# Attention passes of a four-layer graph network: TensorE signals aggregations once a quad, four-head query rows once for eight chunks, and transposed weights together with the factor

## The chip, the cores and the metric

One core of a Trainium2 chip runs the whole program. The metric is the device time of one execution in microseconds (us), lower is better. Engines are named as in the profile: PE is TensorE's matmul, PEld its weight load, DVE VectorE, ACT ScalarE, POOL GpSimd, SP SyncE.

## The reference

A graph with 3125 nodes of 256 features and 53125 edges sorted by destination (`dst`). Four graph layers, each followed by residual and layer norm: a plain sum over edges, two layers of graph attention with four heads, three layers of a graph transformer with eight heads, and a relational sum over edges. The change touches the five attention passes only:

```python
# four heads, two passes
e = leaky_relu(el[src] + er[dst])
ex = exp(e - segment_max(e, dst)[dst])
out = segment_sum(z[src] * (ex / segment_sum(ex, dst)[dst]), dst)
# eight heads, three passes
scores = sum(Q[dst] * typed(K[src]), -1) * mu / sqrt(32)
e = exp(scores - segment_max(scores, dst)[dst])
agg = segment_sum(V[src] * (e / (segment_sum(e, dst)[dst] + 1e-10)), dst)
```

## The kernel before

Edges lie in chunks of 128, one edge in each partition. `attend` handles a window of 16 chunks (`WC`) at a time: 28 windows with four heads ("sums" below, `dots` false), 29 with eight ("dots", `dots` true). A quad is four chunks. A unit is what is aggregated in one PSUM bank: one chunk in sums (16 units in a window, four in a quad, six banks `pp`), two in dots (8 units, two in a quad, three banks).

Window w goes through these steps:

- POOL gathers the table row of each edge by an indirect DMA, one for each chunk (L757), into a ring of windows. Before each quad it waits until the quad that held the place is aggregated (`s_pp`, L749 to L751).
- SP loads the destination rows that become one-hot matrices for eight chunks at a time (L741); ACT turns them into ones and zeros (L855, L858).
- PE brings the query row of each edge (`qrows`: L779 in sums, L785 in dots) and signals `s_q` once a quad. DVE makes scores: `leaky` in sums (L945 to L951), `dot` and `red` in dots (L931, L936).
- PE transposes the scores (`T1`, L793), DVE takes running maxima (`D1` to `D3`), PE makes differences (`below`, L797 and L798) and the ratio between windows (`ratio`, L802), ACT takes exponentials (`weights`, L881 and L882), PE transposes them back (`T5`, L807), and ACT copies them into the ring (L886 and L887 in dots, L889 in sums).
- PE makes the factor that rescales the running sum (`factor`, L813 to L815), ACT copies it (`factors`, L893), and T1 of the next window waits for that copy (`s_fc`).
- ACT makes one-hot matrices for the aggregation (`rows`, L864 and L869), DVE multiplies the gathered rows by the weights (`weigh`, L1010), PE aggregates unit by unit (`agg`, L828) and signals `s_pp` after each unit, and DVE rescales (L1000, L1001) and adds each unit to its tile (`add`, L1018).

All engines run rounds: round r aggregates window r-2, makes the weights of r-1 and the scores of r. The order inside a round is written by hand for DVE and PE. In the strings, for PE, C1 to C5 are `T1`, `below`, `ratio`, `T5` and `factor`, Q and N are query rows of a quad of this and of the next window, and G0 to G7 are eighths of the aggregation (two units in sums, one in dots). For DVE, S is `dot`, R `red`, W `weigh`, t the rescaling, A an add of this round's window, P an add of the window before, L `leaky`, and B a residual. `agg` waits on `s_acc` for a free bank.

A `then_inc` on the last matmul of a group is PE's signal; any engine waits for it with `wait_ge`. The first and the last stage of the program (`sum_edges`, L1144 for its indirect DMAs, L1193 for its matmuls) have the same kind of gather and aggregation without attention. Between the attention passes lie dense stages, in which POOL issues no indirect DMA.

## Time and profile before

| | us |
|---|---|
| median of three runs | 7191.65 |
| lowest and highest | 7173.81, 7196.2 |
| the profiled execution | 7153.48, its span 7151.4 |
| PE, DVE, ACT, POOL busy | 4511.4, 3873.4, 3586.2, 3942.8 |

A row of groups reads: line, engine, operation, output<-input, shape, count | busy us, mean ns of one | idle time of the engine just before them, and what ended it. A row of the timeline reads: start us, duration us, engine, line, operation, and in brackets how long the engine had sat idle. "issue" there means that the profile shows nothing that the engine waited for. "remote", or a DMA named by an old buffer, stands where a wait ended at a time at which no instruction that updates its semaphore had just ended.

### The profile page before, as it was taken

How to read it: one execution, taken by the hardware profiler on the slowest of the kernel's cores; microseconds unless marked ns; L12 is line 12 of the kernel's file. 1: busy time of each engine (PE TensorE's matmuls, PEld its weight loads, DVE VectorE, ACT ScalarE, POOL GpSimd, SP SyncE). 2: the span in 40 equal slices, each digit the busy share in tenths (PEclk: the TensorE clock that was granted, in tenths of full speed). 3: DMA queues.
4: the chain of work that ended last, by engine and by line, in shares of the span. 5: the costliest groups of instructions: out<-in, count | busy, mean ns of one | idle time of the engine just before them, and what ended most of it. 6: DMA issues, size and time to landing. Idle time of an engine off the chain costs nothing. (4 is left out here: it accounts for less than half of the span.)

```text
span 7151.4 us, 82528 instructions
## 1 busy us (share of the span) xinstructions
PE 4511.4 (63%) x22100; PEld 3453.4 (48%) x22100; DVE 3873.4 (54%) x9224; ACT 3586.2 (50%) x9073; POOL 3942.8 (55%) x3964
## 2 busy tenths in 40 slices
PE   5444355445556456655777895777895777895444
PEld 3344233323444244454555784555794555673332
DVE  7222223245667356675777445777545777663223
ACT  3333132334444444455666575666575666555554
POOL 0666566647773677535666225666225666215665
PEclk9555566666777676787888997888897888997666
DMA  1111233333432433336666326666326666423333
GB/s 60 44 50 55 62 97 94 90 94 108 110 109 63 115 108 110 90 125 196 196 193 193 90 79 192 195 195 194 91 79 185 192 194 193 114 89 118 92 90 90
DMA packets 395658, 864.23 MB, mean 121 GB/s; under 512 B 93353, under 2 KB 203851, under 8 KB 391763
## 3 DMA queue, kind: packets, MB, share of 16 engines
q0 software_dynamic: 209680, 608.73, 31.4%
q1 hardware_dynamic: 177296, 246.02, 10.3%
q10 hardware_dynamic: 8243, 4.30, 0.2%
q8 instruction: 193, 3.16, 0.2%
q14 instruction: 246, 2.02, 0.1%
HBM read 743.33 MB, written 115.44 MB: 120 GB/s over the span
## 5 line engine op out<-in xcount | busy, mean ns | idle before, releaser
L757 POOL DMA_INDIRECT ring<-tab_kv,idx_i x1044 | 1072.5, 1027 | 534.2 <-issue 295.7
L757 POOL DMA_INDIRECT ring<-tab_z,src_i x880 | 948.8, 1078 | 402.0 <-issue 243.2
L1193 PE MATMUL pp<-ring,oh 128*128 128x256 f32 x1760 | 609.0, 502 | 635.8 <-issue 268.6
L1018 DVE TENSOR_TENSOR acc<-acc,pp 128x264 f32 x1576 | 668.3, 424 | 470.9 <-PE pp L828 120.7
L1327 DVE TENSOR_TENSOR acc<-acc,pp 128x256 f32 x880 | 370.5, 421 | 889.2 <-DMA tab_z<-zs 280.4
L1193 PEld LDWEIGHTS pp<-ring,oh 128*128 128x128 f32 x1760 | 416.2, 251 | 829.1 <-issue 677.3
L828 PE MATMUL pp<-ring,scratch 128*128 128x264 f32 x1760 | 678.5, 526 | 114.2 <-issue 66.7
L785 PE MATMUL pq<-Qs,oht 128*128 x4176 | 620.5, 306 | 186.4 <-issue 98.2
L828 PE MATMUL pp<-ring,X 128*128 128x264 f32 x2088 | 667.4, 454 | 51.0 <-DVE acc L1018 32.0
L1010 DVE TENSOR_TENSOR ring<-ring 128x1024 f32<-128x1024 f32 x481 | 585.9, 1219 | 187.7 <-ACT ring L889 108.6
L785 PEld LDWEIGHTS pq<-Qs,oht 128*128 128x128 bf16 x4176 | 439.3, 109 | 346.6 <-issue 238.1
L638 POOL DMA_INDIRECT rec<-R,idx_i x416 | 408.2, 981 | 274.5 <-DVE idx_i L613 142.4
L1144 POOL DMA_INDIRECT ring<-tab_y,src_i x440 | 417.9, 950 | 237.5 <-issue 123.0
L1144 POOL DMA_INDIRECT ring<-tab_h,idx_i x440 | 420.6, 956 | 224.3 <-issue 121.4
L828 PEld LDWEIGHTS pp<-ring,scratch 128*128 128x128 f32 x1760 | 401.5, 255 | 256.1 <-issue 125.2
L855 ACT ACTIVATE oht<-oht,part_c 128x1024 bf16<-128x1024 bf16 x284 | 323.3, 1138 | 401.2 <-DMA oht<-lo_row_p 197.2
L931 DVE TENSOR_TENSOR X<-ring,pq 128x1024 f32<-128x1024 f32 x261 | 317.6, 1217 | 346.7 <-issue 252.4
L828 PEld LDWEIGHTS pp<-ring,X 128*128 128x128 f32 x2088 | 423.3, 223 | 157.2 <-issue 44.3
L757 POOL DMA_INDIRECT H<-tab_kv,idx_i x348 | 351.7, 1011 | 235.0 <-issue 84.6
L864 ACT ACTIVATE X<-iota_row,lo__40877 128x128 f32<-128x128 f32 x1392 | 424.1, 388 | 2.4 <-PE pp L828 2.4
L936 DVE TENSOR_REDUCE scw<-X 128x32 f32<-128x1024 f32 x348 | 422.9, 1215 | 0.8
L1685 POOL TENSOR_TENSOR R<-H,rows 128x256 f32<-128x256 f32 x75 | 66.0, 880 | 586.1 <-DVE H L2070 586.1
(363 smaller groups left out, 9421.3 us busy)
## 6 DMA issues: line engine op xcount, KB each, us to landing
oht<-lo_row_p SPq DMA_DIRECT2D x174, 256.0 KB
oht<-lo_row_s SPq DMA_DIRECT2D x110, 256.0 KB
drow<-in_dst SPq DMA_DIRECT2D x25, 1024.0 KB
tab_h<-hs SPq DMA_DIRECT2D x25, 1024.0 KB, 4.4
tab_kv<-X SPq DMA_DIRECT2D x50, 396.0 KB, 2.7
tab_kv<-X SPq DMA_DIRECT2D x50, 384.0 KB, 3.4
ring<-tab_kv,idx_i POOLq DMA_INDIRECT x1044
ring<-tab_z,src_i POOLq DMA_INDIRECT x880
```

The lines of the kernel that those rows point to most:

```text
L638: nc.gpsimd.indirect_dma_start(out=rec, out_offset=bass.IndirectOffsetOnAxis(ap=slot[:, j:j + 1], axis=0), in_=R[:, j, :], in_offset=None) ...
L757: nc.gpsimd.indirect_dma_start(out=one(w, c, 0, row), out_offset=None, in_=table, in_offset=bass.IndirectOffsetOnAxis(ap=idx[:, w * WC + c ...
L785: last = nc.tensor.matmul(o, lhs, Qs[:, bass.ds(tile_, 1), r, :].rearrange("p a d -> p (a d)"), start=(r == 0), stop=(r == 2))
L828: last = nc.tensor.matmul(pp[(w * NU + n) % NB][:, 0:W8], oh[:, w % 2, UC * n + c, :], one(w, UC * n + c, 0, W8), start=(c == 0), stop=(c ...
L855: nc.scalar.activation(oht[:, k % LOB, :], oht[:, k % LOB, :], ACT.Abs, scale=-1.0, bias=part_c[:, :]).then_inc(s_ac, 1)
L864: last = nc.scalar.activation(oh[:, w % 2, c, :], iota_row[:, :], ACT.Abs, scale=-1.0, bias=lo_s[:, w * WC + c:w * WC + c + 1])
L936: nc.vector.tensor_reduce(scw[:, w % 2, :, 4 * q:4 * q + 4].rearrange("p h c -> p c h"), prod[:, q % 2, :, :].rearrange("p c (h x) -> p c ...
L1010: nc.vector.tensor_tensor(v, v, bc(ex, 3, D // heads), ALU.mult).then_inc(s_m, 1)
L1018: nc.vector.tensor_tensor(a, a, pp[(w * NU + p) % NB][:, 0:W8], ALU.add).then_inc(s_acc, 1)
L1144: nc.gpsimd.indirect_dma_start(out=ring[:, b, k, c, :], out_offset=None, in_=table, in_offset=bass.IndirectOffsetOnAxis(ap=idx[:, 2 * p + ...
L1193: last = nc.tensor.matmul(bank[:, c * D:(c + 1) * D], oh[:, b, 2 * k + c, :], ring[:, b, k, c, :], start=True, stop=True)
L1327: nc.vector.tensor_tensor(a, a, pp[b % 2 * BP + k][:, c * D:(c + 1) * D], ALU.add).then_inc(s_v, 1)
```

## The change

PE signals `s_pp` after the last unit of a quad only: 4 times in a window instead of 16 in sums, instead of 8 in dots. Every waiter counts quads instead of units: POOL's gathers, ACT's `rows`, DVE's `add`. In sums `s_q` is signalled after every second quad. T5 does not signal any more, `factor` does not wait for ACT's copy, and ACT waits once, for the factor, then copies the transposed weights and the factor. `T5` and `factor` stand next to each other in PE's order, ahead of G5 in dots and of G6 in sums. In DVE's order for sums, four adds instead of six are left for the next round.

```diff
-    ORDER_V_SUMS = order("W0 P10 P11 W1 P12 P13 W2 P14 P15 t D1 A0 A1 D2 A2 A3 D3 A4 A5 W3 B A6 A7 A8 A9 L")
-    ORDER_T_DOTS = order("l C1 G0 Q2 G1 G2 Q3 G3 C2 C3 G4 C4 G5 C5 N0 G6 N1 G7")
-    ORDER_T_SUMS = order("l G0 C1 G1 Q0 Q1 G2 Q2 Q3 G3 G4 C2 C3 G5 C4 G6 C5 G7")
+    ORDER_V_SUMS = order("W0 P12 P13 W1 P14 P15 W2 t D1 A0 A1 D2 A2 A3 D3 W3 A4 A5 B A6 A7 A8 A9 A10 A11 L")
+    ORDER_T_DOTS = order("l C1 G0 Q2 G1 G2 Q3 G3 C2 C3 G4 C4 C5 G5 N0 G6 N1 G7")
+    ORDER_T_SUMS = order("l G0 C1 G1 Q0 Q1 G2 Q2 Q3 G3 G4 C2 C3 G5 C4 C5 G6 G7")
...
-                            e.wait_ge(s_q, 2 * (k - LOB + 1))
+                            e.wait_ge(s_q, (2 if dots else 1) * (k - LOB + 1))
...
-                                e.wait_ge(s_pp, (w + 3 - RW) * NU + QU * (q + 1))
+                                e.wait_ge(s_pp, (w + 3 - RW) * NQ + q + 1)
...
-                        last.then_inc(s_q, 1)
+                        if dots or q % 2:
+                            last.then_inc(s_q, 1)
...
-                        nc.tensor.transpose(ex_t, S1, ident[:, :]).then_inc(s_T5, 1)
+                        nc.tensor.transpose(ex_t, S1, ident[:, :])
                     def factor(w):
-                        e.wait_ge(s_ex, w + 1)
...
-                        last.then_inc(s_pp, 1)
+                        if n % QU == QU - 1:
+                            last.then_inc(s_pp, 1)
...
-                        e.wait_ge(s_pp, w * NU + HU * (h + 1))
+                        e.wait_ge(s_pp, w * NQ + NQ // 2 * (h + 1))
...
-                        e.wait_ge(s_T5, w + 1)
+                        e.wait_ge(s_fac, w + 1)
                         ex = ex_t.rearrange("p (h c) -> p c h", h=HD)
...
-                    def factors(w):
-                        e.wait_ge(s_fac, w + 1)
                         nc.scalar.copy(facs[:, w % 2, :], fac).then_inc(s_fc, 1)
...
-                        e.wait_ge(s_q, w * NQ + quads(w))
+                        e.wait_ge(s_q, 2 * w + quads(w) // 2)
...
-                        e.wait_ge(s_pp, w * NU + (p + 1 + 2 * NU))
+                        e.wait_ge(s_pp, (w + 2) * NQ + p // QU + 1)
```

## Rows read from the trace of the kernel before

**Rows 1.** The page: busy time of each engine over the whole span.

```profile
PE 4511.4 (63%) x22100; PEld 3453.4 (48%) x22100; DVE 3873.4 (54%) x9224; ACT 3586.2 (50%) x9073; POOL 3942.8 (55%) x3964
```

**Rows 2.** Windows: stretch, length, then PE, PEld, DVE, ACT, POOL busy, clock, DMA.

```profile
1640.00:2260.00 620.00, 382.74 (x1609) 267.82 (x1609) 396.92 (x1009) 303.93 (x680) 412.77 (x376) 0.74 0.39 103
3300.00:3960.00 660.00, 497.87 (x2530) 367.73 (x2529) 508.96 (x945) 409.24 (x1163) 431.63 (x421) 0.83 0.69 192
```

**Rows 3.** Windows, POOL alone: gathers of two sums, one dots, the last stage.

```profile
1560.00:2229.00 669.00, 471.38 (x436) 0.70 0.41 109
2337.00:3001.00 664.00, 472.89 (x440) 0.69 0.41 111
3236.00:3948.00 712.00, 472.53 (x464) 0.81 0.69 194
6479.00:7100.00 621.00, 413.92 (x433) 0.66 0.32 91
```

**Rows 4.** Groups of POOL's gathers: sums, dots (two), last stage.

```profile
L757 POOL DMA_INDIRECT ring<-tab_z,src_i x436 | 471.4, 1081 | 192.3 <-issue 121.1 <-remote 41.4 <-PE pp L828 29.9
L757 POOL DMA_INDIRECT ring<-tab_kv,idx_i x348 | 356.2, 1024 | 184.7 <-issue 99.9 <-DMA keep_link<-link_p 38.8 <-POOLq L150 17.8
L757 POOL DMA_INDIRECT H<-tab_kv,idx_i x116 | 116.4, 1004 | 72.6 <-issue 28.6 <-PE pp L828 25.7 <-DMA keep_link<-link_p 15.2
L1144 POOL DMA_INDIRECT ring<-tab_h,idx_i x425 | 406.3, 956 | 219.7 <-issue 117.2 <-DMA tab_z<-zs 74.5 <-SPq L1097 15.5
```

**Rows 5.** Timeline of one round of sums, from the ratio on.

```profile
1838.71 0.20 PE L802 MATMUL pc<-G,one_c 128*1 128x8 f32 x2
1838.84 1.16 PE L828 MATMUL pp<-ring,scratch 128*128 128x264 f32 x4
...
1847.57 0.95 POOL L757 DMA_INDIRECT ring<-tab_z,src_i  x1 [0.30 <-issue]
1850.08 0.28 ACT L881 ACTIVATE scratch<-pc 128x128 f32<-128x128 f32 x1 [8.54 <-remote]
...
1850.45 0.48 PE L807 MATMUL pc<-ident,scratch 128*128 128x128 f32 x1 [10.46 <-issue]
...
1851.62 1.69 POOL L757 DMA_INDIRECT ring<-tab_z,src_i  x1 [3.10 <-remote]
```

**Rows 6.** Timeline of one round of sums, the factor and its copy.

```profile
1723.26 0.57 PE L815 MATMUL pc<-gr,scratch 1*128 1x8 f32 x2
...
1732.79 0.17 ACT L893 COPY facs<-pc 128x8 f32<-128x8 f32 x1 [10.46 <-remote]
```

**Rows 7.** Timeline of a dense stage, where POOL issues no indirect DMA.

```profile
4100.09 1.03 PE L1716 MATMUL pbe<-Wo,xa 128*128 128x256 f32 x4
...
4101.16 0.42 DVE L2011 TENSOR_TENSOR H<-pbe,H 128x256 f32<-128x256 f32 x1 [2.45 <-PE pbe L1716]
```

**Rows 8.** Timeline of one round of dots around the factor.

```profile
3461.03 1.73 PE L828 MATMUL pp<-ring,X 128*128 128x264 f32 x4
...
3462.74 0.42 DVE L1018 TENSOR_TENSOR acc<-acc,pp 128x264 f32 x1
...
3463.06 0.38 PE L813 MATMUL pc<-one_r 1*128 1x8 f32 x2 [0.30 <-issue]
3463.08 1.22 DVE L936 TENSOR_REDUCE scw<-X 128x32 f32<-128x1024 f32 x1
...
3463.53 0.36 PE L815 MATMUL pc<-gr,X 1*128 1x8 f32 x2
...
3468.46 0.17 ACT L893 COPY facs<-pc 128x8 f32<-128x8 f32 x1 [5.46 <-DMA keep_x<-H]
3468.49 0.43 DVE L1018 TENSOR_TENSOR acc<-acc,pp 128x264 f32 x1 [4.20 <-DMA keep_link<-link_p]
```

More of the change, by code:

```diff
@@ L724, in attend @@
             ratio_row, fac = pc[0:1, 3 * P:3 * P + HD], pc[:, 3 * P + HD:3 * P + 2 * HD]
-            (s_go, s_oh, s_ev, s_q, s_mul, s_red, s_T1, s_G, s_Gm, s_eg, s_T5, s_fac, s_fc, s_ex, s_m, s_pp,
+            (s_go, s_oh, s_ev, s_q, s_mul, s_red, s_T1, s_G, s_Gm, s_eg, s_fac, s_fc, s_ex, s_m, s_pp,
              s_acc, s_d, s_ma, s_ab, s_ac, s_max) = (s.sem(n) for n in (
-                 "go", "oh", "ev", "q", "mul", "red", "T1", "G", "Gm", "eg", "T5", "fac", "fc", "ex", "m", "pp",
+                 "go", "oh", "ev", "q", "mul", "red", "T1", "G", "Gm", "eg", "fac", "fc", "ex", "m", "pp",
                  "acc", "d", "ma", "ab", "ac", "max"))
@@ L748, in _ @@
                             if dots and w >= RW - 1:
-                                e.wait_ge(s_pp, (w + 3 - RW) * NU + QU * (q + 1))
+                                e.wait_ge(s_pp, (w + 3 - RW) * NQ + q + 1)
                             elif w >= RW:
-                                e.wait_ge(s_pp, (w + 2 - RW) * NU + QU * (q + 1))
+                                e.wait_ge(s_pp, (w + 2 - RW) * NQ + q + 1)
                             if dots and w:
@@ L763, in _ @@
                 def _(e):
-                    e.sem_inc(s_pp, 2 * NU)
+                    e.sem_inc(s_pp, 2 * NQ)
                     def tiles(w):
@@ L897, in _ @@
                     for r in range(nw + 2):
-                        if r >= 2:
-                            factors(r - 2)
                         if 0 < r <= nw:
```

## Prediction, made before the changed kernel was run

> **What bounds the kernel now.** I read the page first. No engine is busy for more than 63% of the span [rows 1], so the time lies in waits between engines and the stage must be read by itself. The windows of the attention stages say the same: in a stretch of 620 us of sums, POOL is busy for 413 us, DVE 397, PE 383 and ACT 304; in 660 us of dots DVE is busy for 509, PE 498, POOL 432, ACT 409 [rows 2]. So nothing is full, and I ask who sets the pace.
>
> The pace can be counted in gathers. The gathers of the first sums pass take 669 us for 436 (1.53 us each), of the second 664 for 440 (1.51), of a dots pass 712 for 464 (1.53), and of the last stage, whose aggregation has no attention around it, 621 for 433 (1.43) [rows 3]. POOL itself would go faster: 0.95 us for a plain gather and 0.30 before the next, thus 1.25 [rows 5]. The groups show what is lost. In a sums pass POOL idles 192.3 us, of which 121.1 is that regular "issue"; 71 us are waits for aggregations. In a dots pass it is 257.3, less 128.5 of issue: 129 us [rows 4]. So POOL is no fixed bound; it is held by rounds of about 24.5 us (16 gathers by 1.53), in which DVE is busy for 19 us in dots and 16 in sums (by its shares [rows 2]).
>
> What makes a round long is seen in the timeline. The ratio matmul ends at 1838.91. ACT, which waits for its signal, starts at 1850.08 after 8.54 us of idle time. In between PE has ended its aggregations (at 1840.00) and has nothing to do for 10.46 us, and POOL issues gathers until 1848.52. POOL then stops, because it waits for an aggregation that PE had also ended by 1840.00, and after that all three go on [rows 5]. The factor shows the same: it ends at 1723.83, ACT's copy starts at 1732.79 [rows 6], 8.96 us later. In a dense stage, where there are no indirect DMAs, PE ends at 4101.12 and DVE starts at 4101.16 [rows 7]. So **a signal of PE arrives microseconds late while POOL issues gathers**, and only signals of PE have this in the rows I looked at. In dots, PE's factor ended at 3463.89 and its fifth aggregation at 3462.76, and both waiters started at 3468.46 and 3468.49 [rows 8]: two signals with different semaphores come out together, as from one queue. That the queue lets signals out in order, so that a signal that nobody needs delays the next one, is my reading of this, not a row.
>
> **The change part by part.** *Fewer signals.* In a window of sums PE signals 24 times (16 units, 4 quads of query rows, T1, ratio, T5, factor); 12, 2 and 1 go, 9 stay. In dots it is 16 (8, 4, 4), and 4 and 1 go, 11 stay. Over two passes of 28 windows, the last one half empty, 826 go, over three of 29, 435. The price of one on the path lies between 0.04 us [rows 7] and 11.2 us [rows 5], so a product says nothing. What bounds the gain is the pace. If late signals stopped mattering beyond what the last stage has, each pass would run at its 1.434 us a gather: 436 by 0.100 is 44 us and 440 by 0.075 is 33 us for sums, 464 by 0.100 is 47 us for each dots pass. Together that is 77 + 140 = 217 us. I take the last stage and not POOL's own 1.25 us as the floor, since it has only 8 signals of PE for 16 gathers, fewer than 9 or 11, and yet idles 219.7 - 117.2 = 102 us on 425 gathers [rows 4]: few signals don't remove that loss. If POOL's waits went wholly, it would be 2 by 71 plus 3 by 129, 529 us; nothing in the rows supports that much.
>
> The Trainium skill weighs the same thing and comes out elsewhere. TensorE: Matmul & The Clock Gate, section "The cost: per-tile semaphore tail", says that increments on completion serialize at about 26 ns each and that a single one on the last matmul is sound. By it, 1261 signals fewer would be worth 33 us at most, an estimate from that page. The trace does not agree on the size: the lateness is some 9 to 11 us [rows 5, 6].
>
> *Sums: the chain of a round.* Before the ratio's signal in a round stand those of the query rows and of six or eight aggregated units; with the change about three. After it, T5's and the factor's signal become one. ACT's copy of the weights now waits for the factor's six small matmuls too (0.38 + 0.36 + 0.36 us at full clock, about 0.8 in all by their starts [rows 8]) but not for a second late signal, and T1 of the next window gets `s_fc` earlier. On DVE, `leaky` stands behind two more adds (2 by 0.43 [rows 8], and what each waits for the one before), but those two no longer stand at the head of the next round, so DVE's sum is unchanged; A8 to A11 wait for G5, which PE runs behind the ratio. Queued behind them are only `leaky` and T1. I expect the chain to get shorter than the gathers' pace and take two thirds of the 77 us: **50 us**.
>
> *Dots: a tighter coupling.* Two costs stand against five signals fewer. G5 now stands behind T5 and the factor on PE, and A4 waits for G5 instead of G4. Queued behind A4 on DVE is the last `red`, for which PE's next T1 waits. In one round [rows 8] A4 started at 3462.74, 20 ns before G5 ended, and `red` at 3463.08 hid in a wait that lasted until 3468.49. With the change A4 itself waits for that signal and `red` (1.22 us) comes after it; and the factor's 0.8 us comes ahead of G5, together 2.0 us in such a round. Where the weights come in time, A4 waits less or not at all: 0 to 2.0 us, and ahead of A0 and A2 there is work on DVE that hides the quad. A gain of less than nothing is thus possible. Against it stands what is to be had, 1.6 us a round (140 over 87), since one fewer signal after the ratio comes early for ACT and three to five fewer keep the queue short. I take 0.4 us net a round, nearer to nothing because the two sizes are close: **35 us** over 87 rounds.
>
> *Start and end of a pass.* While POOL fills the ring of four windows, nothing makes it stop, and signals of the first rounds come late. Fewer of them may bring 0 to 10 us a pass; I take 2 by 5, **10 us**, for sums, where the cut is deepest, and nothing for dots. SP's transfers wait for `s_q` at the same count of query rows as before, so they and POOL's places keep their moments; nothing moves past them. The removed instructions themselves (a wait of T5's, one of `factor`) stand in idle time of PE and ACT: nothing.
>
> The sum is 50 + 35 + 10 = 95 us, thus 7153.5 - 95 = 7058 us for the profiled execution. The median lies 38 us above that execution (7191.65 against 7153.48), so the median becomes **7097 us**.
>
> **The rivals.**
>
> *The whole gap to the last stage's pace goes.* For it: every pass has its signals cut to about what that stage has, and the largest loss shown is a signal, not work [rows 5]. Against: the coupling in dots [rows 8]. 7191.65 - 217 = 6975 us.
>
> *The burst of gathers sets the lateness, not the number of signals.* Everything is released only after POOL has stopped [rows 5]. If signals are held until then whatever their number, POOL stops as often and as long as before, and the change is worth the merged wait alone. For it: the last stage idles 102 us with few signals. Against: the factor's copy starts at 1732.79 while POOL goes on gather after gather [rows 6]. This is also the case in which the change does not do what it says. From the rows I give it 0 to 15 us: 7185 us. By the rule of the Trainium skill above, the result would lie between this case and the forecast, at 7159.
>
> *Slower: A4 and the factor in dots.* If A4 waits in every round and the quad's signal is still late, the 2.0 us of above come whole, 87 by 2.0 = 174 us, less the 60 of sums and less what fewer signals give in dots, at 0.4 to 1 us a round. It decides from where the coupling costs over 0.7 us a round net, since 87 by 0.7 eats the 60 us. With 1.3 us net: 113 - 60 = 53 us slower, 7245 us.
>
> **How the numbers follow.** My forecast, from 7050 to 7170, has 0.50, the whole gap 0.18, the held signals 0.16, the slower dots 0.16. A measurement of this kernel can tell about 0.3% from no change, so "the same" is 7170 to 7213. Of the forecast 0.03 falls into it, of the held signals 0.12 (0.03 below, 0.01 above), of the slower dots 0.03. Faster: 0.47 + 0.18 + 0.03 = 0.68. The same: 0.03 + 0.12 + 0.03 = 0.18. Slower: 0.01 + 0.13 = 0.14. The range should leave two tenths out: 6985 below cuts half of the whole-gap case, 7225 above cuts two thirds of the slower one.
>
> **What would show it.** In the changed profile, the pace of gathers in sums should fall from 1.53 and 1.51 to about 1.45, in dots from 1.53 to about 1.51, and the last stage should stay at 1.43. POOL's idle time beyond "issue" in a sums pass should fall from 71 to under 50 us. ACT's waits for the ratio of several microseconds should get rarer, and those before the factor's copy should vanish as a group, since it stands behind the copy of the weights. In dots I look at the adds that start after G5: if A4 has an idle time before it of over 2 us in most rounds, with `red` behind it, the coupling is real. The prediction is wrong if the rounds of sums don't shorten (then the number of signals is not the cause) or if dots lengthen by more than 0.7 us a round.

## The result, and the profile after

| | before, us | after, us |
|---|---|---|
| median of 14 runs each | 7181.53 | 7157.51 |
| lowest and highest | 7154.79, 7196.2 | 7132.8, 7176.04 |
| profiled execution | 7153.48 | 7134.54, its span 7132.4 |

The ratio of after to before is 0.9969, with a 95% interval of 0.9957 to 0.9981: 22 to 24 us faster, where 95 were forecast. The two profiled executions differ by 19 us.

The windows of POOL, over two sums passes, one dots pass and the last stage (stretch, length, POOL busy and gathers, clock, DMA share, GB/s), stand against [rows 3]:

```profile
1560.00:2206.00 646.00, 470.21 (x433) 0.68 0.42 111
2320.00:2970.00 650.00, 468.36 (x433) 0.70 0.41 112
3199.00:3918.00 719.00, 481.95 (x463) 0.81 0.69 192
6465.00:7090.00 625.00, 414.74 (x434) 0.69 0.32 91
```

Sums went from 1.53 and 1.51 us a gather to 1.49 and 1.50, dots from 1.53 to 1.55, the last stage stayed (1.44). The groups of POOL's gathers over the same stretches answer to [rows 4]:

```profile
L757 POOL DMA_INDIRECT ring<-tab_z,src_i x433 | 471.3, 1088 | 176.1 <-issue 124.2 <-DMA keep_link<-link_p 33.2 <-PE pp L828 18.6
L757 POOL DMA_INDIRECT ring<-tab_kv,idx_i x348 | 364.2, 1047 | 195.1 <-issue 96.6 <-remote 55.4 <-PE pp L828 18.3
L757 POOL DMA_INDIRECT H<-tab_kv,idx_i x115 | 118.3, 1029 | 59.1 <-remote 28.0 <-issue 27.4 <-PE pp L828 3.7
L1140 POOL DMA_INDIRECT ring<-tab_h,idx_i x434 | 414.9, 956 | 210.4 <-issue 121.6 <-DMA tab_z<-zs 70.6 <-PE pp L1189 18.2
```

In sums POOL's waits fell from 71 to 176.1 - 124.2 = 52 us. In dots they didn't: 195.1 + 59.1 - 96.6 - 27.4 = 130 us, 129 before, and the gathers themselves took 482.5 us instead of 472.6.

Whole passes, from the first gather to the last add (us, worked out from the starts and ends in the two traces):

| | sums 1 | sums 2 | dots 1 | dots 2 | dots 3 |
|---|---|---|---|---|---|
| before | 728.0 | 725.7 | 746.1 | 747.6 | 752.7 |
| after | 708.5 | 714.1 | 760.2 | 752.5 | 749.9 |

Sums gained 31 us, dots lost 16, the rest of the program gained 4: the 19 us. This is one execution of each kernel; more traces of either code come with the experiments, and there the loss in dots doesn't stand out from the scatter. The signals still come late. In one round of dots (timeline: start, duration, engine, line, operation, idle time before it):

```profile
3701.99 0.28 ACT L882 ACTIVATE X<-pc 128x128 f32<-128x128 f32 x1 [3.91 <-remote]
3702.03 0.43 DVE L1014 TENSOR_TENSOR acc<-acc,pp 128x264 f32 x1 [4.61 <-remote]
...
3702.70 0.94 POOL L757 DMA_INDIRECT ring<-tab_kv,idx_i  x1 [2.41 <-remote]
...
3714.53 0.43 DVE L1014 TENSOR_TENSOR acc<-acc,pp 128x264 f32 x1 [3.67 <-remote]
3714.87 1.22 DVE L932 TENSOR_REDUCE scw<-X 128x32 f32<-128x1024 f32 x1
```

ACT, DVE and POOL go on within 0.7 us of each other after 2.4 to 4.6 us of idle time, as in [rows 5] and [rows 8]. At 3714.53 an add waits 3.67 us with `red` behind it, the coupling that I had priced.

**Two measures that the experiments use.** *Lateness*: the trace records updates of semaphores (about four fifths of PE's); set in order against the ends of PE's signalling matmuls, they give how late each signal came. Before: 2.5 us on average in sums, 2.1 to 2.3 in dots. After: 2.3 to 2.4 and 1.8 to 2.0. PE signals 0.98 times a microsecond in sums before and 0.38 after, and the lateness of one hardly changed. Signals of DVE and ACT are 0.01 us late throughout. Held signals come out in bursts, some 40 to 60 ns apart (that they keep their order is assumed in the matching, not shown by it).

The longest hold that I found stands in the kernel before, in the first round of the first sums pass:

```profile
1582.80 0.20 PE L802 MATMUL pc<-G,one_c 128*1 128x8 f32 x2
...
1620.39 0.95 POOL L757 DMA_INDIRECT ring<-tab_z,src_i  x1 [0.30 <-issue]
1621.23 0.28 ACT L881 ACTIVATE scratch<-pc 128x128 f32<-128x128 f32 x1 [27.52 <-remote]
...
1621.65 0.95 POOL L757 DMA_INDIRECT ring<-tab_z,src_i  x1 [0.30 <-issue]
```

The ratio matmul ends at 1583.00, ACT is free from 1593.71 and starts at 1621.23, 38 us after the end of what it waits for. All this time POOL issues a gather every 1.25 us, and it goes on after it: a hold can end without POOL having stopped.

*Idle time before the adds A0 to A7 of a round of dots*, mean us:

```
           A0    A1    A2    A3    A4    A5    A6    A7    sum
before    0.00  0.15  0.10  0.77  0.11  0.94  1.31  0.00   3.4
after     0.00  0.00  2.29  0.00  1.80  0.00  1.84  0.00   5.9
```

### The profile page after: what moved, and what is told of

The parts are those of the page before. It is cut to its first block and busy times, and to the rows that moved or that the text cites. A ratio compares the mean times of both kernels' runs of the same rounds, so it can differ in the third digit from the quotient of the medians.

```text
span 7132.4 us, 82385 instructions
## 1 busy us (share of the span) xinstructions
PE 4578.5 (64%) x22100; PEld 3490.1 (49%) x22100; DVE 3868.9 (54%) x9224; ACT 3568.6 (50%) x9073; POOL 3980.4 (56%) x3964
## 5 line engine op out<-in xcount | busy, mean ns | idle before, releaser
L757 POOL DMA_INDIRECT ring<-tab_kv,idx_i x1044 | 1097.4, 1051 | 571.2 <-issue 287.0
L1014 DVE TENSOR_TENSOR acc<-acc,pp 128x264 f32 x1576 | 669.0, 424 | 822.7 <-DMA keep_link<-link_p 144.5
L828 PE MATMUL pp<-ring,X 128*128 128x264 f32 x2088 | 706.7, 471 | 131.0 <-DVE acc L1014 100.2
L785 PEld LDWEIGHTS pq<-Qs,oht 128*128 128x128 bf16 x4176 | 453.8, 111 | 321.0 <-issue 200.3
L1140 POOL DMA_INDIRECT ring<-tab_h,idx_i x440 | 420.7, 956 | 227.4 <-issue 123.1
L927 DVE TENSOR_TENSOR X<-ring,pq 128x1024 f32<-128x1024 f32 x261 | 317.1, 1215 | 128.1 <-DMA ab<-in_L_gnn_ar 62.4
```

Of the source, the lines that this page charges most:

```text
L757: nc.gpsimd.indirect_dma_start(out=one(w, c, 0, row), out_offset=None, in_=table, in_offset=bass.IndirectOffsetOnAxis(ap=idx[:, w * WC + c ...
L785: last = nc.tensor.matmul(o, lhs, Qs[:, bass.ds(tile_, 1), r, :].rearrange("p a d -> p (a d)"), start=(r == 0), stop=(r == 2))
L828: last = nc.tensor.matmul(pp[(w * NU + n) % NB][:, 0:W8], oh[:, w % 2, UC * n + c, :], one(w, UC * n + c, 0, W8), start=(c == 0), stop=(c ...
L1014: nc.vector.tensor_tensor(a, a, pp[(w * NU + p) % NB][:, 0:W8], ALU.add).then_inc(s_acc, 1)
L1140: nc.gpsimd.indirect_dma_start(out=ring[:, b, k, c, :], out_offset=None, in_=table, in_offset=bass.IndirectOffsetOnAxis(ap=idx[:, 2 * p + ...
```

## The experiments

All times are medians beside runs of the kernel before on the same chip, and the ratio is to those.

| run | this, us | before, us | ratio | 95% interval |
|---|---|---|---|---|
| e1_sums_only | 7098.26 | 7149.04 | 0.9933 | 0.9916 to 0.995 |
| e2_signals_back | 7100.29 | 7149.04 | 0.9926 | 0.9912 to 0.994 |
| e3_pace_after | 7244.91 | 7149.04 | 1.0135 | 1.0119 to 1.0151 |
| e4_pace_before | 7237.63 | 7149.04 | 1.0121 | 1.0105 to 1.0137 |
| e5_after_again | 7147.82 | 7171.2 | 0.9966 | 0.9952 to 0.9981 |
| e6_dots_quad | 7140.72 | 7171.2 | 0.9960 | 0.9944 to 0.9976 |
| e7_dots_merge | 7128.19 | 7171.2 | 0.9943 | 0.9929 to 0.9957 |
| e8_pace4_after | 7140.92 | 7171.2 | 0.9966 | 0.9953 to 0.9979 |
| e9_after_third | 6502.98 | 6432.99 | 1.0101 | 1.0084 to 1.0117 |
| e10_signals_back_again | 6502.29 | 6432.99 | 1.01 | 1.0085 to 1.0116 |
| e11_pace8_sums | 6538.27 | 6432.99 | 1.0157 | 1.0144 to 1.0171 |
| e12_half_rows | 6495.45 | 6432.99 | 1.0092 | 1.0073 to 1.011 |
| e13_after_fourth | 7097.01 | 7149.69 | 0.9928 | 0.9904 to 0.9953 |
| e14_signals_back_third | 7096.51 | 7149.69 | 0.9919 | 0.9898 to 0.994 |
| e15_sums_only_again | 7092.39 | 7149.69 | 0.9921 | 0.99 to 0.9942 |
| e16_half_rows_again | 7197.31 | 7149.69 | 1.0064 | 1.0043 to 1.0086 |
| e17_sums_quad | 7132.02 | 7176.95 | 0.9945 | 0.9926 to 0.9964 |
| e18_sums_merge | 7197.98 | 7176.95 | 1.0033 | 1.0021 to 1.0045 |

The before column holds a surprise of its own: 7149 to 7177 us on four occasions (7182 in the result above), 6433 on one. The runs e9 to e12 were on that chip, called the fast one below; the others are the slow ones. The record gives one and the same chip number to e1 to e4 and to e17 and e18, where the kernel before took 7149 and 7177 us; so a difference of 0.4% between occasions needs no edit.

### Does the number of signals cost?

Theory Q: the queue of PE's signals is served one by one, so each signal that nobody needs delays the rest. Rival: the gathers hold the queue, however long it is. The experiment keeps the changed kernel and puts every removed signal back, on a semaphore that nobody waits for (826 + 435 = 1261 of them).

```diff
-                        if dots or q % 2:
-                            last.then_inc(s_q, 1)
+                        last.then_inc(s_q if dots or q % 2 else s_x, 1)
...
-                        nc.tensor.transpose(ex_t, S1, ident[:, :])
+                        nc.tensor.transpose(ex_t, S1, ident[:, :]).then_inc(s_x, 1)
...
-                        if n % QU == QU - 1:
-                            last.then_inc(s_pp, 1)
+                        last.then_inc(s_pp if n % QU == QU - 1 else s_x, 1)
```

> The full change, but each signal that it removed is put back on its matmul with a semaphore that nobody waits for: the number of PE signals is that of before (24 and 16 a window), who waits for what is as in the change. Theory Q (signals leave PE in order through a queue, so each one delays those behind it): rounds get longer than in the change by what the cut brought and more, since the quad's signal now stands behind up to three others; over 30 us slower than the change, 7190 us or more. Theory B (a burst of gathers sets how late signals are, whatever their number): the same as the change within 10 us, 7150 to 7165 us.

> The change with its removed signals put back for nobody, now on one chip with the change itself. On its own chip it came out at 0.9926 of before, the change at 0.9966 and 0.9969 on two others. If the number of signals costs nothing: between 0.993 and 0.997, equal to the change within 0.2%. If it costs as I forecast: slower than the change by 0.4% or more. That idle signals make the kernel faster would have no mechanism of mine.

> The change with its removed signals put back for nobody. Where signals are in time this was equal to the change (6502.3 against 6503.0 us). Where they are late: if their number matters through a queue in order, slower than the change by 0.4% or more; if the burst of gathers alone sets the lateness, equal within 0.2%; if it is faster by 0.4%, as 0.9926 against 0.9966 on different chips would have it, then fewer signals themselves are harmful.

e2 had no run of the changed kernel beside it, so it was repeated with one: e10 beside e9 gave 6502.29 against 6502.98 us, e14 beside e13 7096.51 against 7097.01. 1261 more signals cost -0.7 and -0.5 us; the four and six executions of each kernel leave room for a cost of some 10 us in either pair, not for 0.4% (26 and 28 us). In e14's trace PE signals as often as in the kernel before (1.05 a microsecond in sums) and the mean lateness is 1.6 to 2.4 us in sums and 1.2 to 1.8 in dots, against 2.2 to 2.4 and 1.7 to 1.8 in e13's on the same chip. **Theory Q falls**, on which my sum was built. The Trainium skill's rule (TensorE: Matmul & The Clock Gate, "The cost: per-tile semaphore tail") had given an estimate of 33 us at most for them; the runs show none of it.

### Do the gathers hold the signals?

POOL gets a pause after each gather in both kernels, a small `memset` and a wait for it, in the attention passes alone.

```diff
                                     ).then_inc(s_g[w % RW][q], 16)
+                                nc.gpsimd.memset(idle_[:, :], 0.0).then_inc(s_idle, 1)
+                                paced[0] += 1
+                                e.wait_ge(s_idle, paced[0])
```

> The full change with a pause on POOL after every gather of the attention passes: a memset of 128x64 and a wait for its end, some 0.2 to 0.4 us, so gathers are issued every 1.45 to 1.65 us instead of 1.25. Theory P (signals of PE get late only because POOL issues faster than something behind it takes, about 1.43 us a gather in the last stage): the late signals go away, PE to ACT and DVE are prompt as in the dense stages, rounds become as long as 16 gathers at the new pace. With 1.45 us: 16 by 1.45 = 23.2 us against 24.6, 5 by 28 by 1.4 = up to 190 us faster than the change. With 1.65 us: 26.4 us a round, some 230 us slower, but with prompt signals. Rival (any gather delays signals, at any pace): signals stay late by 2 us on average, and the pause adds to every round.

> The kernel before with the same pause on POOL after every gather of the attention passes. Theory P: prompt signals, and with them the number of signals costs nothing, so this is as fast as the changed kernel with the pause within 10 us. Theory Q: with 24 signals a window against 9, this is slower than the changed kernel with the pause by more than 20 us.

The windows of POOL alone, one sums and one dots pass, of the paced changed kernel and then of the paced kernel before:

```profile
1538.00:2245.00 707.00, 530.89 (x879) 0.70 0.40 105
3250.00:3990.00 740.00, 546.96 (x927) 0.81 0.70 187
```

```profile
1546.00:2261.00 715.00, 538.85 (x879) 0.71 0.40 104
3277.00:4011.00 734.00, 540.97 (x927) 0.83 0.70 189
```

Half of the instructions are pauses, so a gather comes every 707/440 = 1.61 us and 740/464 = 1.59. The mean lateness is 0.01 to 0.07 us in the one and 0.01 to 0.15 in the other, from 2 and more. The factor and the copy of the weights, which waits for its signal, in the paced changed kernel:

```profile
1909.92 0.57 PE L821 MATMUL pc<-gr,scratch 1*128 1x8 f32 x2
...
1910.53 0.27 ACT L896 COPY ring<-pc 128x128 f32<-128x128 f32 x1 [1.94 <-issue]
```

PE ends at 1910.49 and ACT starts at 1910.53, where the factor's own copy came 8.96 us late in [rows 6]. **So PE's signals are held by gathers issued back to back, and a slightly slower POOL frees them**, with 24 signals a round or with 9. The cure costs more than the illness, since a gather now comes every 1.6 us. The pair also prices the two kernels with prompt signals: 7244.91 against 7237.63. By passes the paced changed kernel is 8.9 and 8.8 us shorter in sums and 8.8, 6.2 and 3.1 longer in dots.

A rarer pause, every fourth gather:

```diff
+                                if c % 4 == 3:
+                                    nc.gpsimd.memset(idle_[:, :], 0.0).then_inc(s_idle, 1)
```

> The changed kernel with a pause on POOL after every fourth gather only (memset of 128x64, wait for its end). In the kernel with a pause after each gather the pitch was 1.39 us within a quad, with 0.5 and 0.9 us more at two places of four, 1.60 on average, and PE's signals were late by 0.01 to 0.07 us on average instead of 2. With one pause in four the pitch should be 1.35 to 1.45 us. Theory P: if the average pitch is at or above 1.43, signals are prompt and the passes take 640 and 665 us for the gathers instead of 657 and 718, 100 to 250 us faster than before in all. If a quad's own burst of four at 1.25 us is enough to make signals late: between 0 and 50 us faster than the change.

It came out as the changed kernel beside it (7140.92 against 7147.82 us, inside the intervals), at the "0 to 50 us" of the second case and not at the 100 to 250 of the first. In sums the signals were prompt (0.12 us) and the tail of a pass shortened to 37 us from 53, but the gathers took 679 us:

```profile
1558.00:2237.00 679.00, 488.89 (x549) 0.73 0.42 109
3220.00:3934.00 714.00, 491.98 (x579) 0.80 0.70 194
```

In dots this pause was too short: lateness 1.6 to 2.3 us at 714/464 = 1.54 us a gather, less than the pause of every gather needed.

### A chip on which nothing is late

> The changed kernel once more, as the one beside which the next three run. 0.997 of before again.

Neither theory had this: the kernel before took 6433 us on that chip and the changed kernel was 1.0% slower. The windows of POOL of the changed kernel there, one sums and one dots pass, and its group of gathers in sums:

```profile
1352.00:1979.00 627.00, 493.21 (x440) 0.74 0.45 118
2910.00:3539.00 629.00, 480.35 (x464) 0.81 0.78 219
```

```profile
L757 POOL DMA_INDIRECT ring<-tab_z,src_i x440 | 494.7, 1124 | 141.9 <-issue 132.0 <-POOLq L150 8.1 <-PE pp L828 1.8
```

POOL waits for PE 1.8 us in a whole sums pass, a dots pass runs at 1.36 us a gather, and the mean lateness is 0.01 us in all five passes, without any pause. In the last stage, whose code is the same in both kernels, the page of the changed kernel on this chip and on the first one:

```profile
L1140 POOL DMA_INDIRECT ring<-tab_h,idx_i x440 | 420.8, 956 | 149.2 <-issue 132.2
```

```profile
L1140 POOL DMA_INDIRECT ring<-tab_h,idx_i x440 | 420.7, 956 | 227.4 <-issue 123.1
```

POOL's own work is equal to 0.1 us, but it waits for 17 us here and for 104 there. So what differs between the chips lies behind POOL.

A natural reading is that the slow chips drain the gathers more slowly (1.44 to 1.55 us each by the pace of the stages, against the 1.25 at which POOL issues them), that something fills, and that PE's signals stand behind it. The DMA packets in the traces don't bear it out. In the first sums pass the last packet of a gather ends 1.50 us (median) after POOL's instruction in the kernel before, 1.51 in the paced changed kernel and 1.51 on the fast chip; in the first dots pass it is 2.45, 2.43 and 2.67, in the last stage 1.46 and, on the fast chip, 1.48. In the kernel before it is 1.48 us for the sixteenth gather of a burst as well. So the data don't queue up on the slow chips. What does differ, besides the lateness, is how many updates of the gathers' semaphores the trace holds (each gather makes 16): 1839 of 7040 in that sums pass of the kernel before, 4585 in the paced one, 6931 on the fast chip. This may be a trait of the recording alone. Between the gathers and PE's signals the place of the hold stays open, and so does why one chip doesn't have it.

### Is it the bytes?

Theory D: the gathers' bytes set the dots' pace, so nothing could be had there. The kernel before, with rows of 1056 bytes instead of 2080 in dots (the keys are left out, so it computes something else), and a `memset` of the ring ahead of each pass, about 15 us.

```diff
-                                    out=one(w, c, 0, row), out_offset=None, in_=table,
+                                    out=one(w, c, 0, W8 if dots else row), out_offset=None,
+                                    in_=narrow if dots else table,
```

> The kernel before, but in the eight-head passes each gather brings rows of 264 numbers (1056 bytes) instead of 520 (2080 bytes), from the same table; the keys stay unset, so the scores and the output mean nothing. Same number of gathers, signals and instructions. If dots are held by the bytes of the gathers (theory D: the 1.53 us a gather are the transfer's own pace, so no cut of signals could shorten them): the pace falls to that of sums or below, 1.43 to 1.50 us, each pass 15 to 45 us shorter, and signals less late than 2.2 us. If dots are held by the chain of a round (my forecast's picture): the pace stays at 1.53 us within 0.01.

> The kernel before with gathers of 1056 instead of 2080 bytes a row in the eight-head passes (keys unset, output without meaning), and a memset of the ring of some 15 us ahead of each. Where the kernel before has 1.53 us a gather in dots: theory D (the transfers hold dots) 1.43 to 1.50 us a gather and signals less late; the forecast's picture (the chain of a round holds dots) 1.53 within 0.01. Where signals are in time: 1.34 us a gather as with full rows, since POOL's own 1.25 us and its waits for DVE then hold it.

e12 fell on the fast chip, in two executions, where it could say little on this, and was repeated on a slow one. Two dots passes of e16:

```profile
3249.00:3964.00 715.00, 456.94 (x464) 0.79 0.44 108
4348.00:5070.00 722.00, 463.67 (x464) 0.79 0.44 107
```

107 and 108 GB/s instead of 194 [rows 3], and still 1.54 and 1.56 us a gather (0.01 to 0.03 above 1.53), lateness 1.7 to 2.1 us. **Theory D falls.** Neither the pace nor the hold goes by the byte. Of the 48 us by which e16 as a whole is slower, the three `memset`s take 40 (13.3 each).

### Which part helps, which costs?

In dots: e1 leaves the dots as before, e6 takes the quads alone (T5 and the factor apart, in the old order), e7 the merged signal with its order alone. Sums are changed in all three.

```diff
 e1: quad = merged = False in dots      e6: merged = False in dots      e7: quad = False in dots
+                        if n % per == per - 1:          # per = QU if quad else 1
+                            last.then_inc(s_pp, 1)
...
+                        e.wait_ge(s_fac if merged else s_T5, w + 1)
```

> The change in the two four-head passes alone; the three eight-head passes are as before. The two profiles show sums shorter by 31 us together (passes and their tails) and dots longer by 16 us. If this division is real and not scatter of one execution each: about 31 us under before, thus a ratio of 0.9957, and 15 us faster than the full change. If the scatter of a pass is as large as these differences (the rival): the same as the full change, 0.997.

> The change in sums only. Where signals are late the profiles so far have the change at 9 to 15 us a dots pass above before, which makes this 16 to 40 us faster than the full change (0.9933 of before on another chip). Where signals are in time, dots passes were 655 to 662 us with the old dots and 665 to 669 with the new, so about 28 us faster than the full change.

> Sums as in the change. In dots one signal a quad, but T5 signals by itself, the factor waits for ACT's copy, and G5 stands ahead of the factor, as before. My term for dots had two costs: A4 waits for G5 (red behind it, 1.2 us) and the factor ahead of G5 (0.8 us). If the quad's coupling is what made dots 16 us longer: as slow as the full change or slower. If the merge of T5 and the factor did it: 10 to 20 us faster than the full change, dots 748 us a pass or less.

> Sums as in the change. In dots T5 and the factor are one step with one signal and one wait of ACT, as in the change, but every unit's aggregation is signalled, as before. If the quad's coupling costs in dots: faster than the full change by 10 to 20 us. If the merge costs: as the full change.

Beside the changed kernel's 7147.82, e6 is 7 and e7 20 us faster; e7's interval (to 0.9957) just meets the changed kernel's (from 0.9952), e6 is inside it. In the profiled executions e7's two sums passes are 25 us shorter than those of e5, with the same code, so a lead of this size is not all the edit's. On another chip e15 is 5 us faster than e13, inside the intervals, where 16 to 40 were expected; and e2, which has the changed dots, is level with e1 on theirs (7100.29 and 7098.26).

The traces of the slow chips say the same. The three dots passes take 2236 to 2270 us together in five traces with the changed dots (the changed kernel, e2, e5, e13, e14) and 2242 to 2253 in five with the old ones (the kernel before, e1, e15, e17, e18). The two sums passes take 1404 to 1434 us in nine traces with the changed sums, 1454 in the kernel before and 1461 in e16, which has its sums. **On the slow chips the gain in sums is clear of the scatter, and the loss in dots is not.**

The longer waits are. The adds' idle time is 2.6 to 3.7 us a round in e15's dots passes against 4.9 to 5.0 in e13's. By pass it is 2.5 to 3.1 in the kernel before, 5.5 to 5.7 in the changed one, 3.0 to 3.3 with the quads alone (e6) and 4.2 to 4.4 with the merge alone (e7): the quads add little by themselves, the merge, which puts G5 behind the factor, adds more, and both together most. On the fast chip, with no lateness at all, these waits cost time: the changed kernel waits 1.8 us before A4 and 1.1 to 1.3 before A6, the old dots (e11) 0.03 us or less before any. There a dots pass takes 668.2, 669.0, 665.3 us with the change and 654.8, 661.5, 658.6 without: 27.6 us in three passes. Which of the two parts costs it was not run there.

e11 is the old dots with the changed sums and a pause every eighth gather of sums:

> The change in sums only, dots as before, and in sums a pause on POOL after every eighth gather. With one pause in four the pitch in sums was 1.55 us, PE's signals came in time (0.12 us late on average), the tail after the last gather was 37 us instead of 55, but the gathers took 681 us instead of 656. One pause in eight adds half of that: a pitch of 1.47 us. Theory P: if signals stay prompt, gathers 648 us and tail 37 us, thus 685 us a pass against 704 with the change in sums alone, and the kernel is about 40 us faster than that one, 0.988 of before. If 1.47 us a gather is above what the path takes: signals late as before, 700 us a pass or more, 0.993 to 0.995 of before.

Its sums passes took 697 us each, 31 and 34 more than e9's 666 and 663: where nothing is late a pause only costs.

In sums: e17 takes the quads with the rarer `s_q` and DVE's new order, e18 the merged signal with its order alone. Dots are as before.

```diff
 e17: quad = not dots, merged = False    e18: quad = False, merged = not dots
-    ORDER_V_SUMS = order("W0 P10 P11 W1 P12 P13 W2 P14 P15 t D1 A0 A1 D2 A2 A3 D3 A4 A5 W3 B A6 A7 A8 A9 L")
+    ORDER_V_SUMS = order("W0 P12 P13 W1 P14 P15 W2 t D1 A0 A1 D2 A2 A3 D3 W3 A4 A5 B A6 A7 A8 A9 A10 A11 L")   # e17
-    ORDER_T_SUMS = order("l G0 C1 G1 Q0 Q1 G2 Q2 Q3 G3 G4 C2 C3 G5 C4 G6 C5 G7")
+    ORDER_T_SUMS = order("l G0 C1 G1 Q0 Q1 G2 Q2 Q3 G3 G4 C2 C3 G5 C4 C5 G6 G7")                                # e18
```

> Dots as before. In sums the aggregations are signalled once a quad, the query rows once for eight chunks, and DVE has the new order of adds; T5 signals by itself and the factor waits for ACT's copy, as before. If the merged T5 and factor bring the gain (one late signal of about 2 us fewer in each of 28 rounds by two passes, at most 112 us): 1.000 of before, with the passes at 720 us or more. If the quads bring it (fewer waits on late signals for DVE's adds): 0.993.

> Dots as before. In sums T5 and the factor are one step with one signal and one wait of ACT, next to each other on PE; every unit is signalled and the order of adds is as before. If the merge brings the gain: 0.993 of before, passes of 700 to 710 us. If the quads bring it: 1.000. Where signals are in time (the kernel before at 6433 us), the one that costs is the one above 1.000, by 0.5% if it is the 16 us a pass alone.

Windows of POOL in the first sums pass, e17 and then e18, and ACT's waits in that pass of e18 (engine, what waited, for what: us in total, times, longest):

```profile
1546.00:2201.00 655.00, 488.27 (x440) 0.71 0.43 113
```

```profile
1557.00:2229.00 672.00, 463.59 (x440) 0.70 0.42 110
```

```profile
ACT ring L896 <- remote: 204.4, 22, 15.8
```

e17's sums passes took 715 and 715 us (728 and 726 before), e18's 740 and 738. **The merge by itself costs, the quads with DVE's new order gain.** In e18 ACT starts the copy of the weights 6.2 and 6.3 us (mean of a pass) after the end of the factor, for which it waits there; in the kernel before it is 1.9 and 1.7 us after T5, in the changed one 1.1 and 2.9 after the factor. ACT stands 204 us in front of that copy, 22 times. Both together, as e1 and e15 have them, took 699 to 708 us a pass and 0.67% and 0.79% off the whole, at least as much as the quads alone (0.55%), though on other occasions: the merge doesn't cost beside the quads what it costs alone. Whether the fewer waits or DVE's order do the work in e17 was not separated and stays open.

What the gain is made of can be seen in the ratio's signal. From the end of that matmul to ACT's exponential it takes (median of the 28 rounds, first and second sums pass) 4.8 and 4.5 us in the kernel before and 6.2 and 7.3 in e16, which has its sums; 2.1 and 2.0 in the changed kernel, 2.2 and 2.9 in e17; and with the removed signals put back it is still 2.7 and 2.1 (e2), 3.0 and 1.4 (e14). So the ratio's signal does come earlier, but not because fewer stand ahead of it. In e18 it comes early too (1.5 and 1.7), and the wait has moved to the factor. What an edit changes is which signal of the round falls into a hold; why it falls there is not shown.

### Why sums are slower on the fast chip

No trace of the kernel before was kept from that chip, but e12's sums are its sums, and e12's group of gathers in the first pass stands beside that of e9:

```profile
L762 POOL DMA_INDIRECT ring<-tab_z,src_i x440 | 473.7, 1077 | 141.9 <-issue 128.3 <-POOLq L150 8.1 <-PE pp L834 5.5
```

POOL's idle time is 141.9 us in both; the gathers themselves take 494.7 us instead of 473.7. The timeline of e9 shows what a long gather is:

```profile
1702.31 0.95 POOL L757 DMA_INDIRECT ring<-tab_z,src_i  x1 [0.30 <-issue]
1703.47 1.22 DVE L1006 TENSOR_TENSOR ring<-ring 128x1024 f32<-128x1024 f32 x1
1703.56 1.95 POOL L757 DMA_INDIRECT ring<-tab_z,src_i  x1 [0.30 <-issue]
```

A gather that meets DVE's `weigh` grows from 0.95 to as much as 1.95 us. Of the 440 gathers of e9's first pass, 102 are longer than 1.1 us, and 100 of these lie beside a `weigh`; so do 100 of 102 in e12. The `dot` (L927 in e9) meets 123 gathers of a dots pass without a `weigh` beside them and makes none long. The SBUF — State Buffer page of the Trainium skill, section "SBUF: two separate sides", says that a VectorE operation with two SBUF inputs, started first, shuts a GpSimd operation that reads SBUF out of a shared port pair for its whole length. `weigh` reads both its inputs from the ring in SBUF, `dot` reads one of its own from PSUM, and a gather takes its indices from SBUF (`src_i`), so the trace agrees: up to 1.0 us more beside 1.22 us of `weigh`. In e9 75 of the 102 took over 1.7 us, in e12 50: the change moved DVE's order against POOL's, and `weigh` now hits the gathers squarer. What the long gathers have above a plain one of 0.95 us adds up to 75.5 + 72.5 us over the two passes in e9 and 55.9 + 58.2 in e12: 33.9 us more, where the passes are 666.4 + 663.2 - 647.4 - 649.5 = 32.7 us longer. The two sizes agree; no run moved `weigh` alone. With the 27.6 us of dots it makes 60 of the 70 us by which e9 is slower. On the slow chips the same is there (471 us of gathers in the first sums pass in [rows 3] and 464 in e18's, 488 in e17's), where POOL waits as well, so a longer gather need not lengthen the pass.

The two paced kernels bear it out with the other sign: there `weigh` happens to hit less in the changed one, 38.9 + 37.4 us above 0.95 against 47.0 + 45.0, 15.7 us less, and its sums passes are 17.7 us shorter. So where signals are prompt, the sums go by where DVE's order lets `weigh` fall among the gathers, and by nothing else that I found.

### The changed kernel on other chips

> The changed kernel itself once more, beside the next three on one chip, so that they are compared with it and not across chips. It should come out at 0.997 of before, as it did; if it comes out at 0.993 as the sums alone and the signals put back did on their chip, then those two showed the chip and not their edit.

> The changed kernel, beside the next three on one chip. Where the kernel before takes 7150 us or more: 0.997 of before and signals late by 2 us. Where it takes 6430 us: 1.010 and no signal late.

0.9966 on one, 0.9928 on the other (below the expected 0.997, and its interval ends below that of the first result), 1.0101 on the fast one. On the chip of 0.9928 the two sums passes took 1411.7 us (e13), against 1460.6 with the old sums (e16): 49 us less, where the first pair of traces had 31. No kernel here beats the rest everywhere: on the slow chips the changed sums with the old dots (0.9933, 0.9921) or with the merge in dots (0.9943) are level with or ahead of the change, on the fast one the kernel before is ahead of all that ran.

## Why the prediction was right in sign and wrong in size

- **"A signal of PE arrives microseconds late while POOL issues gathers": right** (e3, e4: prompt as soon as POOL pauses), and by up to 38 us. It holds on every chip that was tried but the fast one.
- **"A signal that nobody needs delays the next one", which I had called my reading and no row: wrong.** Held signals come out together, as from one queue, but 1261 more of them cost nothing (-0.7 and -0.5 us, e10 and e14). This was the step that failed, and what signalling less often brings came by another way than forecast: that the sign came true is partly luck, and on the fast chip it didn't. My rival, the held signals (7185 us, chance 0.16), had the mechanism, and its 0 to 15 us for what is left was too small, since the change gained 22 to 24 us by other ways.
- **Sums, 50 + 10 us: 31 measured in the first pair of traces, 49 on the chip of e13 and e16.** The size was not far off, its reason was. I had put few signals ahead of the ratio's; that signal does come earlier, 2.1 us instead of 4.8 before ACT goes on, but it does so with all the signals put back as well (2.7, e2). I had taken two thirds of the gap to the last stage's 1.434 us a gather; the passes reached 1.49 (1.47 in e13). What they gained comes from the quads with DVE's order (-0.55%, e17), and the chain argument for the merged signal fails by itself (+0.33%, e18): the copy of the weights waited for a signal that came later, which I had priced at 0.8 us of PE and nothing for lateness (ACT starts it 6.2 us after the factor).
- **Dots, 35 us: nothing gained.** The first pair of traces has 16 us lost, but over five traces of either code on the slow chips the changed dots (2236 to 2270 us) and the old ones (2242 to 2253) overlap; on the fast chip 27.6 us were lost. I had set 0 to 2.0 us of coupling against 1.6 us to be had and taken 0.4 net. The coupling was real: the adds' waits grew by 2.5 us a round in the pass tabled above, as the price foresaw in kind, and on A2 and A6 as well as on A4 (2.29, 1.84 and 1.80 us; A4's is over 2 us in 15 of 29 rounds, where the sign to look for was most of them). I had written that work on DVE hides the quad ahead of A2; with late signals it doesn't. The other side, 1.6 us, was not there: nothing approached the last stage's pace. Why 2.5 us more of waits cost no more than 0.2 us a round where signals are late was not tested.
- **The slower case** (7245 us) has a wait that is there, but of the 113 us that it had for dots at most 16 appear on the chips that the forecast was for. On the fast chip the kernel did get slower, by 27.6 us in dots and 33 in sums, and for the sums no case had a reason.
- **The last stage as a floor** was the second weak step. It told that few signals don't cure the wait, which I had written down, and then I still took its pace for the goal of two thirds of the gap. Its waits are 104 us on one chip and 17 on another with the same code, so they too come from the hold or what causes it, and a dots round has the coupling on top.
- **The profile's signs:** POOL's waits in sums 71 to 52 us (under 50 expected), gathers in sums 1.49 (1.45), dots 1.55 (1.51), last stage 1.44 (1.43).

## What to carry to other kernels

When signals come late, ask by one experiment what holds them before counting them: put the removed ones back where nobody waits, and pace the engine that is suspected. Signalling less often is not free on the waiters' side, since every wait gathers on the first use of a group; check which of them had slack. Ask also for the packets of the transfers before blaming them: here they kept up while the signals did not. And measure a change of some tenths of a per cent on more than one chip, and several traces of either code: here the sign of the whole turned with the chip, and the division by stages of one pair of traces did not hold.

## What the runs showed of the hardware

- On all chips that were tried but one, PE's signals are held for 2 us on average, and up to 38 us (kernel before, first sums round), while POOL issues indirect DMAs back to back at 1.25 us each, and hardly (0.01 to 0.15 us) when they come every 1.6 us (e3, e4). Signals of DVE and ACT, at the same time, are 0.01 us late. 1261 more PE signals change nothing that can be measured (e10, e14).
- The transfers themselves keep up: the last packet of a gather ends a median 1.50 us after POOL's instruction in a sums pass where signals are late, 1.51 where they are not (kernel before, e9).
- The pace doesn't go by the byte: gathers of 128 rows come every 1.54 to 1.56 us with rows of 1056 bytes (e16) and every 1.53 to 1.55 with rows of 2080 (kernel before).
- The same kernel takes 7149 to 7182 us on some chips and 6433 on another. In the last stage, where both kernels have the same code, POOL's own work is equal (420.8 and 420.7 us) and its waits are 17 instead of 104 us (e9, changed kernel).
- A VectorE multiply of two SBUF tensors (1.22 us) lengthens an indirect DMA's issue beside it from 0.95 to as much as 1.95 us, and on the fast chip 34 us more of such lengthening go with passes 33 us longer, of 1300 (e9, e12); a multiply with one input in PSUM lengthens none of 123.
